# Expert loop written out, with eight gathered tiles and six sets of weights

## The chip, the cores and the metric

The kernel runs on one core of a Trainium2 chip. Its time is the device time of one execution in microseconds; the time before is the median of three runs. The profile is that of one further execution.

## The reference

Four layers follow one another, each added to a residual stream of 2 x 1024 tokens of 512 floats: attention with 16 heads, a feed-forward layer with FP4 weights, a linear recurrence, and a mixture of experts. The change touches the last alone:

```python
E, CAP, TOP_K, H, F = 64, 128, 6, 512, 352
scores = softmax(x @ gate_w.T)                    # in float32
topk_w, topk_idx = top_k(scores, TOP_K)
# the first CAP tokens that chose expert e stand in buf[e]; further ones are dropped
g = silu(einsum('ech,ehf->ecf', buf, w_gate))
u = einsum('ech,ehf->ecf', buf, w_up)
d = einsum('ecf,efh->ech', g * u, w_down)
y = sum over a token's six experts of topk_w * d  # zero where it was dropped
y = y + (silu(x @ sh_gate.T) * (x @ sh_up.T)) @ sh_down.T
```

Everything is float32.

## The kernel before

Six phases run one after the other, with a barrier of all engines between them: qkv, attention, FP4 feed-forward, recurrence, router with the shared expert, and the experts. The first five end near 1330 us of the profiled execution, and the change doesn't touch them. The router phase leaves the normalised token rows with their 64 scores behind them in DRAM (tensor xs, in the trace expert_rows: rows of XS = 576 floats), the result so far in DRAM (out, in the trace out_x), and in slot_rows, for each expert, the 128 rows of its slots. It also loads the weights of experts 0 and 1 (PREFETCHED = 2).

experts_phase (L1765) works on one expert after the other, in a step on each engine. The steps run at different times on different engines; semaphores tie them. With e the expert:

- POOL gathers the 128 rows of expert e into xg with an indirect DMA (L1842; row numbers from row_in), AHEAD = 4 experts ahead. When y of expert e is ready and the addition of expert e-1 has landed, it issues the scatter that adds y to out in DRAM, an indirect DMA with compute_op add (L1850; row numbers from row_out), and only then gathers for e+4 into the xg from which y(e) took its scores. The scatter's instruction on POOL raises add_begun; its landing raises added.
- SP loads the weights of expert e (2.16 MB in four DMAs: w_gate and w_up at L1399, w_down at L1404 and L1405) into one of R = 4 sets. It waits until the up product, the split of w_down and the beginning of the addition of expert e-4 are past (three waits, and then all four DMAs). The first loads also wait for three gathers.
- PE, in step e: four transposes of xg(e+1) into a bank (L1866, turn_x); gate, then up of expert e, four float32 products each, which the trace shows as eight matmul records each (L1886); the down product of expert e-1, three float32r products for each of three slices of F (L222 to L224, helper product3); three transposes of hidden(e) (L1895).
- ACT: silu of the gate bank (L1914); the high part of w_down (L1918); weigh(e-1), which writes y, in the trace e_y, from the down bank times the token's score (L1908); the high part of the turned hidden (L1924).
- DVE: copies the turned x out of its bank (L1943), copies a column of slot_rows to row_in for e+4 and to row_out for e (L1934, L1938), multiplies silu and up (L1954), and takes the low parts of w_down and the turned hidden (L1958, L1963).

There are two buffers each of xt, silu, hidden, the split parts and y. Function over_experts writes the first four and the last four steps out, and runs the 56 between in a hardware loop (Fori) of 14 rounds of four steps; in the loop waits against register values go through wait_apart (L411). Steps are numbered by the expert of their gate product, 0 to 63.

Of the kernel before, what the change touches and what calls it, by code (L numbers as in the profile page):

```python
# [13 lines left out]
P = 128  # L14
# [393 lines left out]


def wait_apart(engine, semaphore, value, passed):  # L410


    if not isinstance(value, int):
        value = engine.to_reg(value)  # L414
    engine.wait_ge(passed, 1)
    need(engine, semaphore, value)
# [978 lines left out]
def load_gate_up(sp, a, weights, e, loaded):  # L1395

    for w, name in zip(weights, ("w_gate", "w_up")):
        src = a[name][bass.ds(e, 1)].rearrange("o (p k) n -> p (o k) n", p=P)
        sp.dma_start(w[:, :, :], src).then_inc(loaded, 16)  # L1399


def load_down(sp, a, weights, e, loaded):
    w, src = weights[2], a["w_down"][bass.ds(e, 1)]
    sp.dma_start(w[:, 0:DOWN_FULL, :], src[:, 0:DOWN_FULL * P, :].rearrange("o (k p) n -> p (o k) n", p=P)).then_inc(loaded, 16)  # L1404
    sp.dma_start(w[0:F - DOWN_FULL * P, DOWN_FULL, :], src[:, DOWN_FULL * P:, :].rearrange("o p n -> p (o n)")).then_inc(loaded, 16)  # L1405
# [358 lines left out]
def experts_phase(nc, m, a):  # L1764
# [26 lines left out]
    y = [arena.put(f"e_y{i}", [P, D], F32) for i in range(2)]  # L1791
# [6 lines left out]
    gathered = [s(f"gathered{i}") for i in range(R)]  # L1798
# [6 lines left out]
    def exists(e):  # L1805
        return not isinstance(e, int) or 0 <= e < E

    def over_experts(engine, step):

        for e in range(R):  # L1810
            step(e, e, 0)
        with engine.Fori(1, GROUPS - 1) as g:
            for u in range(R):
                step(g * R + u, u, g)
        for e in range(E - R, E):
            step(e, e % R, GROUPS - 1)

    with nc.Block() as block:

        @block.sync  # L1820
        def _(sp):
            def step(e, u, g):
                if isinstance(e, int) and e < PREFETCHED:
                    return
                if isinstance(e, int) and e == PREFETCHED:
                    for i in range(R - 1):
                        sp.wait_ge(gathered[i], 16)

                need(sp, up_done, e - R + 1)
                need(sp, down_ready, e - R + 1)  # L1830
                need(sp, add_begun, e - R + 1)
                load_gate_up(sp, a, weights[u], e, gu_loaded[u])
                load_down(sp, a, weights[u], e, down_loaded[u])
            over_experts(sp, step)

        @block.gpsimd
        def _(pool):
            def gather(e, u):

                need(pool, y_ready, e - R + 1)  # L1840
                wait_apart(pool, row_in_ready, e + 1, row_in_ready)
# [3 lines left out]
            def step(e, u, g):  # L1845
# [15 lines left out]
        def _(pe):  # L1861
            def turn_x(e, u, g):
                pe.wait_ge(gathered[u], 16 * (g + 1))
# [5 lines left out]
            def down(e, u, g):  # L1869
# [3 lines left out]
                b = u % 2  # L1873
# [4 lines left out]
            def step(e, u, g):  # L1878
                if exists(e + 1):
                    turn_x(e + 1, (u + 1) % R, g if u < R - 1 else g + 1)  # L1880
                pe.wait_ge(xt_ready, e + 1)
                need(pe, gu_loaded[u], 32 * (g if u < PREFETCHED else g + 1))
                need(pe, hidden_ready, e - 1)
                for w, bank, done in ((w_gate, GATEB, gate_done), (w_up, UPB, up_done)):
                    for k in range(KT):
                        last = pe.matmul(m.bank[bank[u % 2]][:, 0:F], xt[u % 2][:, k, :], w[u][:, k, :],  # L1886
                                         start=(k == 0), stop=(k == KT - 1))
                    last.then_inc(done, 1)
                if exists(e - 1):
                    down(e - 1, (u - 1) % R, g if u else g - 1)  # L1890
                pe.wait_ge(hidden_ready, e + 1)
                need(pe, ht_ready, e)
                for k in range(GF):
                    r = rows[k]
                    last = pe.transpose(m.bank[HB][0:r, k * P:(k + 1) * P], hidden[u % 2][:, k * P:k * P + r], m.ident[:, :])  # L1895
                last.then_inc(h_turned, 1)

            turn_x(0, 0, 0)
            over_experts(pe, step)
            down(E - 1, R - 1, GROUPS - 1)  # L1900

        @block.scalar
        def _(act):
            def weigh(e, u):

                act.wait_ge(down_done, e + 1)
                need(act, added, 16 * (e - 1))
                act.activation(y[u % 2][:, :], m.bank[YB[u % 2]][:, :], ACT.Copy,  # L1908
                               scale=xg[u][:, bass.ds(D + e, 1)]).then_inc(y_ready, 1)

            def step(e, u, g):
                act.wait_ge(gate_done, e + 1)
                need(act, hidden_ready, e - 1)
                act.activation(silu[u % 2][:, :], m.bank[GATEB[u % 2]][:, 0:F], ACT.Silu).then_inc(silu_ready, 1)  # L1914
                need(act, down_loaded[u], 32 * (g if u < PREFETCHED else g + 1))
# [130 lines left out]
```

## Time and profile before

| | us |
|---|---|
| median of three runs | 2006.24 |
| lowest and highest | 2005.0, 2006.75 |
| profiled execution, its own time | 2010.12 |
| its span, first to last instruction | 2008.4 |

Busy time and share of the span, from the page:

```profile
PE 1742.8 (87%) x7201; PEld 1211.6 (60%) x7201; DVE 1101.6 (55%) x2379; ACT 693.6 (35%) x1316; POOL 575.7 (29%) x862
```

PE is the matrix engine, PEld its weight load, DVE the vector, ACT the scalar and POOL the GpSimd engine; SP only issues transfers. The page also cuts the span into 40 slices of 50 us: the tenths of each in which PE was busy, TensorE's granted clock in tenths of full speed, and the mean busy share of the 16 DMA engines. The expert loop fills the last 13 or so.

```profile
PE   6997999999888998988599999968888878888786
...
PEclk9996999999999988989799999989889899989888
DMA  6235456655215000000201100158878788787874
```

A share of busy time says little of what sets the pace. That is read from the chain of work that ended last, from the waits of each engine, and from the timeline; a DMA's time is given from its issue to its landing.

### The profile page before, as it was taken

To read this page: it belongs to the slowest core of one execution; us is meant where nothing else is said; L and a number is where in the kernel's file an instruction comes from. 1 tells how busy PE (TensorE), PEld (TensorE's weight loads), DVE (VectorE), ACT (ScalarE), POOL (GpSimd) and SP (SyncE) were. 2 spreads that over 40 slices of the span, in tenths; PEclk is the share of its full clock that TensorE was granted. 3 is DMA by queue.
4 is the path that set the end of the run, shared out by engine and by line. 5 is a ranking of instruction groups with operands and counts; after the bars stand their busy time and mean duration, and the time that the engine had idled before them with its cause. 6 is when DMAs were issued, how large, how long until landed. Compare 5 with 4: busy or idle time off the path is not lost. (4 is left out here: it accounts for less than half of the span.)

```text
span 2008.4 us, 23935 instructions
## 1 busy us (share of the span) xinstructions
PE 1742.8 (87%) x7201; PEld 1211.6 (60%) x7201; DVE 1101.6 (55%) x2379; ACT 693.6 (35%) x1316; POOL 575.7 (29%) x862
## 2 busy tenths in 40 slices
PE   6997999999888998988599999968888878888786
PEld 5884545554466666766477677745555555556564
DVE  5436667766357676765874787763333333333332
ACT  3120555555424534444324222213232223323232
POOL 2003233345503343333541311102222222222222
PEclk9996999999999988989799999989889899989888
DMA  6235456655215000000201100158878788787874
GB/s 246 95 145 154 135 147 169 173 149 150 68 44 195 1 1 1 1 0 21 82 1 62 44 19 35 57 201 268 259 242 284 248 272 269 258 268 242 275 256 130
DMA packets 120637, 284.50 MB, mean 142 GB/s; under 512 B 23456, under 2 KB 35232, under 8 KB 120288
## 3 DMA queue, kind: packets, MB, share of 16 engines
q1 hardware_dynamic: 106208, 247.71, 35.9%
q0 software_dynamic: 14336, 35.66, 8.7%
q8 instruction: 45, 0.74, 0.2%
q14 instruction: 48, 0.39, 0.1%
HBM read 224.03 MB, written 54.69 MB: 139 GB/s over the span
## 5 line engine op out<-in xcount | busy, mean ns | idle before, releaser
L1850 POOL DMA_INDIRECT out_x<-e_y,row_out x64 | 100.8, 1575 | 485.2 <-ACT e_y L1908 481.2
L839 ACT ACTIVATE probs<-bank 128x512 f32<-128x512 f32 (+3 forms) x384 | 167.6, 503 | 194.3 <-PE bank L787 192.8
L1886 PE MATMUL bank<-w_gate,xgt 128*128 128x352 f32 x512 | 208.0, 561 | 0.0
L1954 DVE TENSOR_TENSOR e_hidden<-e_silu,bank 128x352 f32<-128x352 f32 x64 | 33.4, 521 | 269.6 <-issue 219.0
L1105 PE MATMUL bank<-ln_xt_hi,gu_codes 128*128 128x512 f32 x352 | 149.7, 425 | 36.2 <-ACT gate_sum L1120 15.8
L762 PE MATMUL bank<-k_stack,q_stack 96*128 96x512 f32 (+3 forms) x384 | 147.3, 404 | 28.9 <-DMA k_stack<-qk_parts 15.7
L1886 PE MATMUL bank<-w_up,xgt 128*128 128x352 f32 x512 | 163.9, 463 | 0.0
L1866 PE MATMUL bank<-ident,xg 128*128 128x128 f32 x256 | 50.0, 324 | 116.7 <-DMA xg<-expert_rows,row_in 115.9
L1886 PEld LDWEIGHTS bank<-w_gate,xgt 128*128 128x128 f32 x512 | 115.0, 236 | 58.9 <-issue 31.8
L882 DVE CUSTOM_DVE_ANT_0 masked_scores<-bank,wide_mask 128x128 bf16<-128x128 f32 (+3 forms) x256 | 116.2, 483 | 58.1 <-PE bank L762 57.1
L787 PE MATMUL bank<-q_stack,k_stack 98*128 98x512 f32 (+3 forms) x384 | 141.6, 384 | 2.2 <-ACT probs L839 1.8
L801 PE MATMUL bank<-probs,v_ones 128*64 128x512 f32 (+3 forms) x768 | 142.5, 508 | 0.0
L1106 PE MATMUL bank<-ln_xt_lo,gu_codes 128*128 128x512 f32 x352 | 142.0, 403 | 0.0
L1914 ACT ACTIVATE e_silu<-bank 128x352 f32<-128x352 f32 x64 | 29.6, 463 | 324.4 <-PE bank L1886 324.4
L711 POOL TENSOR_SCALAR_AFFINE_SELECT probs<-probs 128x128 f32<-128x128 f32 x256 | 78.3, 322 | 205.7 <-ACT probs L839 201.6
L1886 PEld LDWEIGHTS bank<-w_up,xgt 128*128 128x128 f32 x512 | 101.0, 197 | 58.9 <-issue 8.3
L762 PEld LDWEIGHTS bank<-k_stack,q_stack 96*128 96x128 f32 x384 | 76.8, 202 | 66.5 <-DVE max_parts L882 19.6
L1105 PEld LDWEIGHTS bank<-ln_xt_hi,gu_codes 128*128 128x128 f32 x352 | 67.6, 192 | 81.3 <-ACT gate_sum L1120 21.9
L1958 DVE TENSOR_TENSOR e_down_lo<-w_down,e_down_hi 128x1024 fp32r<-128x1024 f32 (+1 forms) x128 | 116.2, 950 | 0.0
L1866 PEld LDWEIGHTS bank<-ident,xg 128*128 128x128 f32 x256 | 38.0, 210 | 125.1 <-issue 108.1
L1167 DVE SCALAR_TENSOR_TENSOR hidden<-bank,gu_scale,hidden 128x512 f32<-128x512 f32 x132 | 99.0, 750 | 15.5 <-ACT hidden L1120 3.9
L886 DVE TENSOR_REDUCE max_parts<-bank 128x1 f32<-128x512 f32 x128 | 82.5, 683 | 41.8 <-PE bank L762 41.8
(242 smaller groups left out, 3899.1 us busy)
## 6 DMA issues: line engine op xcount, KB each, us to landing
w_gate<-in_w_gate SPq DMA_DIRECT2D x64, 704.0 KB, 5.6
w_up<-in_w_up SPq DMA_DIRECT2D x64, 704.0 KB, 7.6
w_down<-in_w_down SPq DMA_DIRECT2D x64, 512.0 KB, 8.0
q_stack<-qk_parts SPq DMA_DIRECT2D x96, 128.0 KB, 3.9
k_stack<-qk_parts SPq DMA_DIRECT2D x96, 128.0 KB, 4.0
w_down<-in_w_down SPq DMA_DIRECT2D x64, 192.0 KB, 8.5
qk_parts<-qk_stage_hi SPq DMA_DIRECT2D x32, 256.0 KB, 2.0
qk_parts<-qk_stage_lo SPq DMA_DIRECT2D x32, 256.0 KB, 2.3
```

Source lines behind the costliest of these rows:

```text
L762: pe.matmul(m.bank[MAXB[at % 3]][:, 0:cols], qs[slot][j][0:ROWS, q * P:(q + 1) * P], ks[slot][j][0:ROWS, half * CH:half * CH + cols], star ...
L787: pe.matmul(bank[:, 0:cols], ks[slot][j][0:ROWS + 2, k * P:(k + 1) * P], qs[slot][j][0:ROWS + 2, q0:q0 + cols], start=True, stop=True).the ...
L801: pe.matmul(m.bank[OUTB[c]][j * 2 * HD:(j + 1) * 2 * HD, q0 - c * CH:q0 - c * CH + cols], vs[p % 2][j][:, k, :], probs[u % PROBS][:, 0:col ...
L839: act.activation(probs[u % PROBS][:, 0:cols], m.bank[EXPB[u % 3]][:, 0:cols], ACT.Exp, scale=scale).then_inc(exp_ready, 1)
L882: dve.tensor_tensor_reduce(out=masked[at % 4][:, 0:cols], in0=bank[:, 0:cols], in1=wide_mask[:, CH - cols:], scale=1.0, scalar=-3e38, op0= ...
L1105: pe.matmul(bank[:, :], gu[:, k, w], hi[:, k, :], start=True, stop=False)
L1106: pe.matmul(bank[:, :], gu[:, k, w], lo[:, k, :], start=False, stop=True).then_inc(product_done, 1)
L1167: dve.scalar_tensor_tensor(out=total[:, :], in0=m.bank[RING[at % 4]][:, :], scalar=gu_scale[:, half * G0 + g, k:k + 1], in1=total[:, :], o ...
L1850: pool.indirect_dma_start(out=a["out"][:, :], out_offset=bass.IndirectOffsetOnAxis(ap=row_out[u][:, :], axis=0), in_=y[u % 2][:, :], in_of ...
L1866: last = pe.transpose(m.bank[XB][:, k * P:(k + 1) * P], xg[u][:, k:D:KT], m.ident[:, :])
L1886: last = pe.matmul(m.bank[bank[u % 2]][:, 0:F], xt[u % 2][:, k, :], w[u][:, k, :], start=(k == 0), stop=(k == KT - 1))
L1958: last = dve.tensor_tensor(down_lo[u % 2][p, k, :], w_down[u][p, k, :], down_hi[u % 2][p, k, :].bitcast(F32), ALU.subtract)
```

## The change

The hardware loop is gone: each engine's 64 steps are written out, with constants for register values, and wait_apart is no longer needed. Gathers run eight experts ahead (AHEAD = 8, eight xg and row_in); a gather still comes behind the scatter of the expert whose xg it fills. There are six sets of weights (R = 6), and a load waits for up, down split and begun addition of expert e-6; SP asks for the addition first, and for down_ready only between the gate/up and the down loads. There are four y and four row_out (YS = 4), so weigh and the copy to row_out wait for the landed addition of expert e-4. The work of a step and its order on PE, ACT and DVE are as before. Its core:

```diff
+    R, AHEAD, YS = 6, 8, 4
...
-    R = 4
-    GROUPS = E // R
...
-    row_in = [arena.put(f"row_in{i}", [P, 1], U32) for i in range(R)]
-    row_out = [arena.put(f"row_out{i}", [P, 1], U32) for i in range(R)]
-    AHEAD = R
-    xg = [arena.put(f"xg{i}", [P, XS], F32) for i in range(R)]
+    row_in = [arena.put(f"row_in{i}", [P, 1], U32) for i in range(AHEAD)]
+    row_out = [arena.put(f"row_out{i}", [P, 1], U32) for i in range(YS)]
+    xg = [arena.put(f"xg{i}", [P, XS], F32) for i in range(AHEAD)]
...
-    y = [arena.put(f"e_y{i}", [P, D], F32) for i in range(2)]
+    y = [arena.put(f"e_y{i}", [P, D], F32) for i in range(YS)]
+    assert arena.at <= SBUF_END
...
-    def over_experts(engine, step):
-
-        for e in range(R):
-            step(e, e, 0)
-        with engine.Fori(1, GROUPS - 1) as g:
-            for u in range(R):
-                step(g * R + u, u, g)
-        for e in range(E - R, E):
-            step(e, e % R, GROUPS - 1)
+    def loads_of(e):
+
+        return e // R if e % R < PREFETCHED else e // R + 1
 
...
+            for i in range(3):
+                sp.wait_ge(gathered[i], 16)
+            for e in range(PREFETCHED, E):
+                u = e % R
+                need(sp, add_begun, e - R + 1)
                 need(sp, up_done, e - R + 1)
+                load_gate_up(sp, a, weights[u], e, gu_loaded[u])
                 need(sp, down_ready, e - R + 1)
-                need(sp, add_begun, e - R + 1)
-                load_gate_up(sp, a, weights[u], e, gu_loaded[u])
                 load_down(sp, a, weights[u], e, down_loaded[u])
-            over_experts(sp, step)
...
+            def gather(e):
+                u = e % AHEAD
+                need(pool, y_ready, e - AHEAD + 1)
+                pool.wait_ge(row_in_ready, e + 1)
...
-            def step(e, u, g):
-
+            for e in range(AHEAD):
+                gather(e)
+            for e in range(E):
                 pool.wait_ge(row_out_ready, e + 1)
                 pool.wait_ge(y_ready, e + 1)
-                wait_apart(pool, added, 16 * e, row_out_ready)
-                pool.indirect_dma_start(out=a["out"][:, :], out_offset=bass.IndirectOffsetOnAxis(ap=row_out[u][:, :], axis=0),
-                                        in_=y[u % 2][:, :], in_offset=None, compute_op=ALU.add,
+                need(pool, added, 16 * e)
+                pool.indirect_dma_start(out=a["out"][:, :], out_offset=bass.IndirectOffsetOnAxis(ap=row_out[e % YS][:, :], axis=0),
+                                        in_=y[e % YS][:, :], in_offset=None, compute_op=ALU.add,
                                         engine_sem=add_begun).then_inc(added, 16)
-                if exists(e + AHEAD):
-                    gather(e + AHEAD, (u + AHEAD) % R)
-            for e in range(AHEAD):
-                gather(e, e)
-            over_experts(pool, step)
+                if e + AHEAD < E:
+                    gather(e + AHEAD)
             pool.wait_ge(added, 16 * E)
...
-                need(act, added, 16 * (e - 1))
...
+                need(act, added, 16 * (e - YS + 1))
...
-                if not isinstance(e, int) or e >= R:
-                    wait_apart(dve, gathered[u], 16 * g, row_in_ready)
...
-                wait_apart(dve, added, 16 * (e - R + 1), row_in_ready)
...
+                need(dve, gathered[u], 16 * (e // AHEAD))
...
+                need(dve, added, 16 * (e - YS + 1))
```

## Rows read from the trace of the kernel before

**Rows 1.** Table of stretches: length; busy us per engine; clock, DMA share, GB/s.

```profile
1600.00:1700.00 100.00, 82.34 (x311) 57.63 (x310) 36.45 (x80) 28.55 (x58) 25.63 (x20) 0.91 0.81 260
```

**Rows 2.** Chain of work that ended last: start us, us, what ran or landed.

```profile
1582.52 0.70 ACT e_y L1908
...
1586.03 7.17 DMA xg<-expert_rows,row_in
...
1594.07 6.43 PE bank L1886 x16
1602.81 0.70 ACT e_y L1908
```

**Rows 3.** Waits of PE, 1339 to 1985: us in total, times, longest.

```profile
PE bank L1866 <- DMA xg<-expert_rows,row_in: 107.3, 30, 5.4
```

**Rows 4.** Timeline of PE, at steps 1 and 2, within the loop, step 63.

```profile
1346.75 2.53 PE L1886 MATMUL bank<-w_gate,xgt 128*128 128x352 f32 x8
...
1354.39 1.05 PE L1886 MATMUL bank<-w_gate,xgt 128*128 128x352 f32 x3
...
1603.24 2.53 PE L1886 MATMUL bank<-w_gate,xgt 128*128 128x352 f32 x8
...
1613.57 0.75 PE L1866 MATMUL bank<-ident,xg 128*128 128x128 f32 x4 [3.04 <-DMA xg<-expert_rows,row_in]
1614.16 4.22 PE L1886 MATMUL bank<-w_gate,xgt 128*128 128x352 f32 x8
...
1985.23 1.05 PE L1886 MATMUL bank<-w_gate,xgt 128*128 128x352 f32 x3
```

**Rows 5.** Table of stretches, 2 us each, between two bursts and within one.

```profile
1604.00:1606.00 2.00, 2.00 (x8) 1.26 (x8) 1.29 (x5) 0.19 (x1) 1.55 (x1) 1.00 0.00 0
1606.00:1608.00 2.00, 2.00 (x9) 1.26 (x8) 0.00 (x0) 1.73 (x3) 1.01 (x2) 1.00 0.77 86
...
1616.00:1618.00 2.00, 2.00 (x5) 1.21 (x4) 0.00 (x0) 0.00 (x0) 0.00 (x0) 0.50 1.05 387
```

**Rows 6.** Landings: gathers 1400 to 1980; all scatters; those of 1362.89 and 1966.25.

```profile
DMA to landing us min/median/max: 7.1/7.6/9.5
...
DMA to landing us min/median/max: 4.6/5.0/8.7
...
DMA to landing us min/median/max: 6.9/6.9/6.9
...
DMA to landing us min/median/max: 7.6/7.6/7.6
```

**Rows 7.** Weight loads: page's issues; q1 of 1339 to 1987; SP's first issue.

```profile
w_gate<-in_w_gate SPq DMA_DIRECT2D x64, 704.0 KB, 5.6
...
w_down<-in_w_down SPq DMA_DIRECT2D x64, 192.0 KB, 8.5
...
q1 hardware_dynamic: 41664, 134.10, 54.3%
...
q14 instruction: 3, 0.02, 0.0%
...
1339.05 0.34 SPq L1399 DMA_DIRECT2D w_gate<-in_w_gate  x1
```

**Rows 8.** DMA view of 1608 to 1622.6, in a burst: 40 slices, total.

```profile
GB/s 231 328 412 417 417 417 432 412 425 398 421 414 385 379 421 393 404 236 146 129 157 226 286 369 417 386 447 448 359 411 457 436 439 363 375 411 387 415 275 90
DMA packets 1693, 5.25 MB, mean 359 GB/s; under 512 B 188, under 2 KB 188, under 8 KB 1693
```

**Rows 9.** DMA view of 1994 to 2000, a scatter alone; chain's end.

```profile
q0 software_dynamic: 144, 0.26, 34.8%
...
1993.69 4.82 DMA out_x<-e_y,row_out
1998.57 0.71 issue
```

**Rows 10.** DMA view of 1339 to 1987: instruction queue, packets and MB.

```profile
q8 instruction: 3, 0.05, 0.0%
```

More of the change, by code:

```diff
@@ L1867, in turn_x, with down @@
                 last.then_inc(x_turned, 1)
-            def down(e, u, g):
+            def down(e):
                 pe.wait_ge(ht_ready, e + 1)
@@ L1876, in down @@
                           for k, r in enumerate(rows)]).then_inc(down_done, 1)
-            def step(e, u, g):
-                if exists(e + 1):
-                    turn_x(e + 1, (u + 1) % R, g if u < R - 1 else g + 1)
+            turn_x(0)
+            for e in range(E):
+                if e + 1 < E:
+                    turn_x(e + 1)
                 pe.wait_ge(xt_ready, e + 1)
-                need(pe, gu_loaded[u], 32 * (g if u < PREFETCHED else g + 1))
+                need(pe, gu_loaded[e % R], 32 * loads_of(e))
                 need(pe, hidden_ready, e - 1)
@@ L1894, in step, with weigh @@
                     r = rows[k]
-                    last = pe.transpose(m.bank[HB][0:r, k * P:(k + 1) * P], hidden[u % 2][:, k * P:k * P + r], m.ident[:, :])
+                    last = pe.transpose(m.bank[HB][0:r, k * P:(k + 1) * P], hidden[e % 2][:, k * P:k * P + r], m.ident[:, :])
                 last.then_inc(h_turned, 1)
-            turn_x(0, 0, 0)
-            over_experts(pe, step)
-            down(E - 1, R - 1, GROUPS - 1)
+            down(E - 1)
         @block.scalar
         def _(act):
-            def weigh(e, u):
+            def weigh(e):
@@ L1912, in step @@
+            for e in range(E):
                 act.wait_ge(gate_done, e + 1)
                 need(act, hidden_ready, e - 1)
-                act.activation(silu[u % 2][:, :], m.bank[GATEB[u % 2]][:, 0:F], ACT.Silu).then_inc(silu_ready, 1)
-                need(act, down_loaded[u], 32 * (g if u < PREFETCHED else g + 1))
+                act.activation(silu[e % 2][:, :], m.bank[GATEB[e % 2]][:, 0:F], ACT.Silu).then_inc(silu_ready, 1)
+                need(act, down_loaded[e % R], 32 * loads_of(e))
@@ L1916, in step @@
                 need(act, down_done, e - 1)
                 for p, k in TILES:
-                    last = act.activation(down_hi[u % 2][p, k, :], w_down[u][p, k, :], ACT.Copy)
+                    last = act.activation(down_hi[e % 2][p, k, :], w_down[e % R][p, k, :], ACT.Copy)
                 last.then_inc(down_hi_ready, 1)
-                if exists(e - 1):
-                    weigh(e - 1, (u - 1) % R)
+                if e >= 1:
+                    weigh(e - 1)
                 act.wait_ge(h_turned, e + 1)
@@ L1923, in step @@
                 for p, k in TILES:
[L1924 removed]
+                    last = act.activation(ht_hi[e % 2][p, k, :], turned_hidden[p, k, :], ACT.Copy)
                 last.then_inc(ht_hi_ready, 1)
[L1926 to L1927 removed]
+            weigh(E - 1)
         @block.vector
         def _(dve):
[L1931 to L1934 removed]
@@ L1951, in step @@
+            for e in range(AHEAD):
+                copy_row_in(e)
+            copy_x(0)
+            for e in range(E):
+                if e + 1 < E:
+                    copy_x(e + 1)
+                if e + AHEAD < E:
+                    copy_row_in(e + AHEAD)
+                copy_row_out(e)
                 dve.wait_ge(silu_ready, e + 1)
@@ L1962, in step @@
                 for p, k in TILES:
-                    last = dve.tensor_tensor(ht_lo[u % 2][p, k, :], turned_hidden[p, k, :],
-                                             ht_hi[u % 2][p, k, :].bitcast(F32), ALU.subtract)
+                    last = dve.tensor_tensor(ht_lo[e % 2][p, k, :], turned_hidden[p, k, :],
+                                             ht_hi[e % 2][p, k, :].bitcast(F32), ALU.subtract)
                 last.then_inc(ht_ready, 1)
-            for e in range(AHEAD):
-                copy_row_in(e, e, 0)
-            copy_x(0, 0)
-            over_experts(dve, step)
 PHASES = [qkv_phase, attention_phase, ffn_phase, recurrence_phase, router_phase, experts_phase]
```

68 lines of the change are left out of this document (22 added, 46 removed).

## The prediction

> **What bounds the kernel now.** I read the stretch table first: in the expert loop PE is busy 82 us in 100, and the DMA share is 0.81 [rows 1]. Neither is full, so a wait sets the pace. The chain that ended last shows it: the activation that writes e_y, 0.70 us, issue time on POOL and the scatter's own instruction, a gather xg that takes 7.17 us, four transposes, sixteen gate/up matmuls (and, not listed, the down product), and the next e_y [rows 2]. The next e_y comes 20.3 us later, but is that of the second expert after: gather(e+4) is issued behind scatter(e), turn_x(e+4) is step e+3's first work, and down(e+2), also in step e+3, makes y(e+2). One turn of the chain is two experts. The list of PE's waits agrees: 30 waits for xg, 107.3 us, and no other that reaches 1 us in the whole loop [rows 3].
>
> The timeline prices both kinds of step. Without a wait, gate starts 1346.75 and again 1354.39: 7.64 us, with PE always busy [rows 4]. With one, PE stands for 3.04 us in this instance, and the eight gate matmuls after it take 4.22 us in place of 2.53; the granted clock there is 0.50, the lower level, 1.2 GHz [rows 4, 5]. A pair is 2 x 7.64 + 3.04 + 1.69 = 20.0 us, against 20.3 on the chain. From step 1 (1346.75) to step 63 (1985.23) 62 steps take 638.5 us, **10.30 us each** [rows 4].
>
> **The change, part by part.**
>
> Gathers eight ahead, eight xg. Gather(e+8) still follows scatter(e), but has over seven steps until its transposes, some 55 us, against a landing of 9.5 us at the longest [rows 6]. The wait leaves the path for good, with the half-clock gate work after it: up to (10.30 - 7.64) x 62 = **165 us**. That would be all if nothing else came late.
>
> Four more gathers at the start. They are moved ahead of everything POOL does for step 0, some 1.25 us each (0.95 and 0.30 of issue). POOL's first scatter is due at 1355, the four would end at about 1343, and SP's first loads wait for gathers 0 to 2 only, which stay first. Cost on the path: 0. The same bytes, only earlier.
>
> Six sets of weights. Load(e) waits for the addition of expert e-6, which begins near the end of step e-5, so it has four steps, over 30 us, until step e; its parts land 5.6 to 8.5 us after their issue and SP takes about 2 us to issue it [rows 7]. The wait itself costs nothing. What takes its place is the transfers' throughput. SP can now keep up to four sets queued, so the engines should never run dry as they do today.
>
> That capacity is the term that decides. Today bursts of two experts' traffic stand between holes: share 0.00 at 1604 to 1606, 0.77 in the next stretch, and full until the slices fall off near 1622.4 [rows 5, 8]. From about 1606.4 that is 16.1 us for two experts, 8.05 each. The second way: mean share 0.81 x 10.30 = 8.3, a little high, as overlapping packets take some stretches above 1. The third is by parts: one set is 2.16 MB, 134.1 MB for 62 [rows 7]; at the 395 GB/s that loads reach amid a burst (slices of 390 to 430, [rows 8]) 5.5 us. A gather, 128 rows of 576 floats, is 0.295 MB: 0.75 us. A scatter with nothing beside it keeps the engines 34.8% of 6 us, 2.1 us, for 0.26 MB [rows 9]; amid loads it is the dip to some 150 GB/s near 1615 in [rows 8], which gives about 2 us too. Sum 8.3. I take **8.2 us an expert**, the middle of the three. That is above PE's 7.64, so I expect the transfers to bind, and PE to wait some 0.6 us a step for w_gate and w_up, each time far less than the 3.04 us that precede today's slow gate work.
>
> So step 63's weights arrive at 1339.4 (first load issued 1339.05, [rows 7]) + 62 x 8.2 - 1.8 (the last w_down, 0.72 MB, isn't needed for gate) = 1846.0, against 1985.2 today: **139 us** less. Bounds: 8.0 gives 152; 8.5 gives 121. Below 7.64 PE binds and it is 165.
>
> The loop written out. No loop branch and no register waits. A written-out step and a looped one take the same in this trace (head 7.64; looped: 1594.07 to 1603.24 is 9.17, less 1.69 of slow gate 7.5, [rows 2, 4]), so 0 gained. The code must be fetched now: queue q8 moved 3 packets of instructions, 0.05 MB, in the 648 us of the loop [rows 10]; 14 rounds written out may need 14 times as many, 42, and their 0.7 MB are nothing beside 2.7 MB an expert. A late one would stall its engine, and no row here shows a stage with written-out code and full queues. Upper bound: a third of the 42 are PE's and each holds it for the shortest landing of a load, 5.6 us [rows 7], 78 us, of which PE's spare 0.6 us a step (37 us) takes up half: 41 us. Lower bound 0, or a gain of the little that branches cost. I take 0: a fetch needn't wait for anything but its turn, and can be asked for long ahead.
>
> Four y, waits for additions three further back. The scatter itself still waits for the landing of the one before, so additions stay one after another. With idle transfer engines one takes 4.82 us to landing and 0.71 of issue [rows 9], 5.5 us. But the scatters of this loop come in two kinds [rows 6]. The first of a pair meets no loads and lands in 4.6 to 5.1 us. The second is issued into a full burst: asked one by one, the thirty from 1362.89 (6.9 us) to 1966.25 (7.6 us) average 6.84, at most 8.7. From now on all are of the second kind: 6.84 + 0.71 = 7.55 us an addition, below 8.2 but near it. It costs 0 so long as it stays below; four y and row_out let it swing by some steps. DVE's copy of row_out and the ACT activation wait for additions at least four back: 0. SP asks for add_begun before down_ready; when an addition has begun the other is long true, and nothing but loads is queued behind it: 0.
>
> The tail behind step 63's gate start, 23.2 us to the end of the span, stays. **Sum:** 2010.1 (profiled; span 2008.4 and 1.7 around it) - 139 = 1871. The median of the runs lies 3.9 us below the profiled one, so 2006.2 - 139 = **1867 us**.
>
> **The rivals.**
>
> *PE binds (0.13).* If a saturated pair of queues hides part of the scatter, an expert's traffic falls under 7.64 us. For it: 14.6 us of burst moved 5.25 MB at 359 GB/s [rows 8], and 2.72 MB at that rate is 7.6 us. Against: this stretch leaves out most of one scatter. Gain 165: 1841 us, and the clock then stays at 2.4 GHz throughout.
>
> *The chain of additions binds (0.25).* Today's second scatter has an idle stretch of the engines some microseconds on; with queues full all the time each may land like the longer ones. At 8.0 to landing, 8.7 a step, SP's add_begun holds the loads and ACT the y: gain 62 x 1.6 = 99, 1907 us; at the longest, 8.7 and 9.4 a step, gain 56, 1950. For it: the wide spread, 4.6 to 8.7 [rows 6]. Against: these scatters also had the gather of the pair's first expert just ahead, as they will have, and if additions lag, the loads thin out and the landing shortens. The Trainium skill has a rule that speaks for this rival: DMA: Bandwidth & Descriptors, section "Latency and other measured facts", gives the HBM access as 0.2 us on average and 2 us at high load. An add reads and writes HBM, so by it an addition may take up to 3.6 us more than the idle one, 5.5 + 3.6 = 9.1 us (an estimate from the page), and the time would be near 1930; the trace's 2 us between the two kinds of scatter lies within that.
>
> *Slower than before (0.02).* The same place with a higher price: a step costs more than today's 10.30 when a scatter lands in over 9.6 us. The loaded kind is 2 us above the idle one; if a queue of four sets in place of one or two added three times that again, to 12.8 and 13.5 a step, it would be + 62 x 3.2 = 198, 2204 us. None of the 64 scatters is near.
>
> *It doesn't do what it says (0.02).* If gathers still landed late (behind queued loads), PE's waits for xg stay: 2000. They would have to take 55 us.
>
> *Code (0.04).* Instruction fetches late behind full queues, at the upper bound: 1867 + 41 = 1908.
>
> **How the numbers follow.** The forecast, transfers bind at 8.0 to 8.5, has 0.54: 1854 to 1885. The range takes PE's bound (1841) at the low end, and at the high end the code case and most of the addition rival: 1838 to 1920, some 0.85. A difference of 0.2%, 4 us, is about what can be told from no change; every case but two is far beyond it: faster 0.96, same 0.02, slower 0.02.
>
> **What would show it.** Right: PE's wait for xg is gone but for the first; gate starts about 8.2 us apart after a lead of some steps at 7.64; DMA share 0.95 or more through the loop, over 320 GB/s, no holes; PE's remaining waits end on w_gate/w_up loads; granted clock near 1.0; scatters land in about 7 us. Wrong: gate starts 7.64 apart and DMA share below 1 (PE binds); scatter's waits for the landing before it, and SP waiting long for additions (the addition chain); PE idle for "issue" between groups of matmuls (code).

## The result, and the profile after

| | before | after |
|---|---|---|
| median, us | 2006.24 | 1883.96 |
| lowest and highest, three runs | 2005.0, 2006.75 | 1878.89, 1884.23 |
| profiled execution, its span | 2010.12, 2008.4 | 1878.89, 1877.0 |

The changed kernel takes 0.9384 of the time before (95% interval 0.9359 to 0.9409), 122 us less. The forecast was 1867 with a range of 1838 to 1920: the time lies in it, 17 us over the forecast. Started again in a later sitting, the same kernel had a median of 1879.0, so two sittings can differ by 5 us.

First the page: busy time, then three of the lines with 40 slices of 47 us.

```profile
PE 1693.2 (90%) x7201; PEld 1184.8 (63%) x7201; DVE 1097.0 (58%) x2379; ACT 697.1 (37%) x1316; POOL 623.2 (33%) x862
...
PE   6997999999997998898958999999799999999995
...
PEclk9997899999998999998978999999899999999998
DMA  7236356665423200000030021112699999999994
```

In the ten slices before the last, 1361 to 1830 us, TensorE's clock, PE's busy share and the DMA share are all at 9, that is 90% or more; before, the clock fell to 8 in some slices and the DMA share stood at 7 or 8. The table of stretches (columns as in [rows 1]) and the waits (us in total, times, longest) of 1345 to 1830 say what has taken the gather's place:

```profile
1500.00:1600.00 100.00, 93.42 (x388) 65.79 (x386) 43.17 (x96) 37.18 (x72) 40.96 (x24) 1.00 1.00 330
```

```profile
DVE row_out L1908 <- DMA out_x<-e_y,row_out: 220.0, 53, 6.5
POOL out_x L1826 <- DVE row_out L1908: 163.3, 39, 7.0
...
PE bank L1870 <- DVE e_hidden L1927: 21.5, 22, 2.0
```

PE's wait for xg [rows 3] is gone, and the slow gate work behind it. But PE waits for no weights either. What it waits for is e_hidden from DVE, and DVE stands 220 us in front of its copy of row_out, until an addition has landed; SP's waits before it loads, 332.8 us in all, are put down to additions too. The chain that ended last is, from 1500 us on, almost nothing but additions (compare [rows 2]):

```profile
1584.14 0.54 issue
1584.89 5.82 DMA out_x<-e_y,row_out
1590.78 0.54 issue
1591.53 8.99 DMA out_x<-e_y,row_out
1600.58 0.54 issue
1601.33 5.91 DMA out_x<-e_y,row_out
```

One after the other: 0.54 us of issue, 5.8 us to landing, again 0.54, and 9.0. The view of all scatters (duration on POOL in ns min/median/max, start of the first and the last) gives the mean distance from one start to the next: (1867.0 - 1354.1) / 63 = **8.14 us an addition**. Their landings:

```profile
L1826 POOL DMA_INDIRECT out_x<-e_y,row_out x64: 1545/2421/2576, 1354.1 to 1867.0; - x64
...
DMA to landing us min/median/max: 4.7/7.2/9.9
```

In the kernel before a scatter took 1.58 us on POOL, at most 1.62; here the median is 2.42.

```profile
L1850 POOL DMA_INDIRECT out_x<-e_y,row_out x64: 1545/1575/1622, 1355.3 to 1999.3; - x64
```

The timeline around one of the long ones shows its company:

```profile
1584.10 0.15 DVE L1908 COPY row_out<-slot_rows 128x1 uint32<-128x1 uint32 x1 [4.76 <-DMA out_x<-e_y,row_out]
...
1584.21 0.52 DVE L1927 TENSOR_TENSOR e_hidden<-e_silu,bank 128x352 f32<-128x352 f32 x1
...
1584.65 1.82 DVE L1931 TENSOR_TENSOR e_down_lo<-w_down,e_down_hi 128x1024 fp32r<-128x1024 f32 x2
...
1584.89 2.42 POOL L1826 DMA_INDIRECT out_x<-e_y,row_out  x1 [5.29 <-DVE row_out L1908]
...
1587.62 0.99 POOL L1817 DMA_INDIRECT xg<-expert_rows,row_in  x1 [0.30 <-issue]
```

The landing at 1584.1 releases two engines at once. DVE copies row_out, and the hidden product and e_down_lo (1.82 us) come straight behind; POOL issues the next scatter 0.24 us after e_down_lo has begun. 51 of the 64 scatters took more than 1.7 us, and every one was issued while e_down_lo ran.

The 1.82 us of e_down_lo are two instructions, x2 in the row; the view of the tile gives them as 1.22 us (128x1024) and 0.68 us (96x512):

```profile
L1931 DVE TENSOR_TENSOR e_down_lo<-w_down,e_down_hi x128: 678/950/1222, 1344.5 to 1852.1; 128x1024 fp32r<-128x1024 f32 x64, 96x512 fp32r<-96x512 f32 x64
```

The scatter above was issued 0.24 us into the first of the two and ended 1.45 us after that instruction's end.

### The profile page after: what moved, and what is told of

Same layout as the page of the kernel before. It is cut to its first block and busy times, and to the rows that moved or that the text cites. A ratio compares the mean times of both kernels' runs of the same rounds, so it can differ in the third digit from the quotient of the medians.

```text
span 1877.0 us, 22599 instructions
## 1 busy us (share of the span) xinstructions
PE 1693.2 (90%) x7201; PEld 1184.8 (63%) x7201; DVE 1097.0 (58%) x2379; ACT 697.1 (37%) x1316; POOL 623.2 (33%) x862
## 5 line engine op out<-in xcount | busy, mean ns | idle before, releaser
L1826 POOL DMA_INDIRECT out_x<-e_y,row_out x64 | 144.1, 2252 | 310.8 <-DVE row_out L1908 176.2
L1861 PE MATMUL bank<-w_gate,xgt 128*128 128x352 f32 x512 | 163.6, 463 | 0.0
L1908 DVE COPY row_out<-slot_rows 128x1 uint32<-128x1 uint32 x64 | 9.8, 152 | 228.5 <-DMA out_x<-e_y,row_out 228.5
L1861 PEld LDWEIGHTS bank<-w_gate,xgt 128*128 128x128 f32 x512 | 93.8, 193 | 41.4 <-issue 1.3
L778 PEld LDWEIGHTS bank<-q_stack,k_stack 98*128 98x128 f32 x384 | 73.6, 193 | 52.2 <-ACT probs L830 24.9
L1879 ACT ACTIVATE e_y<-bank,xg 128x512 f32<-128x512 f32 x64 | 44.0, 688 | 162.6 <-PE bank L224 162.6
L1889 ACT ACTIVATE e_down_hi<-w_down 128x1024 fp32r<-128x1024 f32 (+1 forms) x128 | 100.0, 832 | 0.0
```

The costliest lines, as they stand in the source:

```text
L778: pe.matmul(bank[:, 0:cols], ks[slot][j][0:ROWS + 2, k * P:(k + 1) * P], qs[slot][j][0:ROWS + 2, q0:q0 + cols], start=True, stop=True).the ...
L1861: last = pe.matmul(m.bank[bank[e % 2]][:, 0:F], xt[e % 2][:, k, :], w[e % R][:, k, :], start=(k == 0), stop=(k == KT - 1))
L1889: last = act.activation(down_hi[e % 2][p, k, :], w_down[e % R][p, k, :], ACT.Copy)
```

## The experiments

Ratios are to the kernel before, on the same chip in the same sitting; "an addition" is the mean distance of the scatters' starts.

| | ratio (95%) | us | an addition |
|---|---|---|---|
| changed kernel, again | 0.9363 (0.9299 to 0.9427) | 1879.0 | 8.10 |
| two_chains | 0.9333 (0.9309 to 0.9357) | 1869.9 | 7.89 |
| loads_free | 0.9624 (0.9587 to 0.9661) | 1930.9 | 8.91 |
| row_out8 | 0.9272 (0.9250 to 0.9294) | 1859.6 | 7.82 |
| written_out | 0.9849 (0.9827 to 0.9871) | 1973.9 | |
| lo_first | 0.9263 (0.9222 to 0.9303) | 1861.9 | 7.81 |
| no_gather | 0.9191 (0.9149 to 0.9233) | 1847.1 | 7.59 |
| ahead8_only | 0.9250 (0.9214 to 0.9287) | 1857.6 | 7.75 |
| sets6_only | 0.9856 (0.9815 to 0.9896) | 1975.9 | |
| ahead8_y4 | 0.9223 (0.9168 to 0.9278) | 1854.6 | 7.80 |
| pace_pe | 0.9592 (0.9526 to 0.9657) | 1921.1 | 8.60 |
| pace_pe_y8 | 0.9480 (0.9415 to 0.9544) | 1904.3 | 8.53 |

The theories: A, the serial additions are the bound; B, the transfer engines' capacity is (the forecast's view); C, it is the place of the wait on DVE, ahead of the hidden product, which holds PE; D, formed from the first results, the wait on DVE makes the additions longer, because it lines e_down_lo up with the next scatter; E, the gather in POOL's queue is what makes every second landing long.

### two_chains: two additions in flight

```diff
-                need(pool, added, 16 * e)
-                pool.indirect_dma_start(out=a["out"][:, :], out_offset=bass.IndirectOffsetOnAxis(ap=row_out[e % YS][:, :], axis=0),
+                need(pool, added[e % 2], 16 * (e // 2))
+                pool.indirect_dma_start(out=a["out" if e % 2 == 0 else "out2"][:, :], out_offset=bass.IndirectOffsetOnAxis(ap=row_out[e % YS][:, :], axis=0),
```

> The changed kernel, but the additions of odd experts go to a second DRAM tensor, which is never merged (that part of the result is left out); so each addition waits only for the landing of the one two experts back, and two are in flight. Same bytes, same loads, same gathers. Theory A (the chain of additions, each waiting for the landing before it, is the bound): gate starts 7.64 us apart almost throughout, DVE's waits on row_out gone, time 1845 to 1855. Theory B (the 16 engines' capacity for this mix of traffic is the bound, and the chain of additions only fills with what they can't do faster): steps stay at 8.1 to 8.2, DMA share 1.0 at some 335 GB/s, time 1870 to 1885.

The odd experts' part of the result is left out here. The time lies between the two forecasts: 9 to 14 us less than the changed kernel. DVE's wait is gone, as A says, but the steps fall only to some 8.0 us. Now ACT does wait for weights, and PE's weight load stands before the gate products, for something that the view can't name ("issue"):

```profile
ACT e_down_hi L1890 <- DMA w_down<-in_w_down: 27.4, 45, 1.2
PEld bank L1862 <- issue: 16.8, 41, 1.4
```

```profile
1600.00:1700.00 100.00, 96.95 (x398) 68.80 (x397) 44.84 (x102) 38.99 (x75) 32.05 (x25) 1.00 1.05 340
```

```profile
DMA to landing us min/median/max: 4.5/9.1/10.9
```

With two additions in flight each lands in 9.1 us, and 340 GB/s is all that passes, though the queue of loads never runs low: from issue to landing a load of w_gate takes

```profile
DMA to landing us min/median/max: 3.9/18.1/21.7
```

against 6.7 us in the changed kernel. So there is a capacity limit close by, at about 8.0 us a step for this order of the traffic. It isn't the changed kernel's: from 1400 us on the engines moved 330 to 334 GB/s there, and the next experiment passed 347 of the same traffic.

### row_out8: DVE's copy waits for an addition eight back

```diff
-    R, AHEAD, YS = 6, 8, 4
+    R, AHEAD, YS, RO = 6, 8, 4, 8
...
-    row_out = [arena.put(f"row_out{i}", [P, 1], U32) for i in range(YS)]
+    row_out = [arena.put(f"row_out{i}", [P, 1], U32) for i in range(RO)]
...
-                need(dve, added, 16 * (e - YS + 1))
-                dve.tensor_copy(row_out[e % YS][:, :], m.slot_rows[:, e:e + 1]).then_inc(row_out_ready, 1)
+                need(dve, added, 16 * (e - RO + 1))
+                dve.tensor_copy(row_out[e % RO][:, :], m.slot_rows[:, e:e + 1]).then_inc(row_out_ready, 1)
```

> The changed kernel with eight row_out in place of four, so that DVE's copy waits for an addition eight back. In the changed kernel DVE stood 228.5 us before this copy, with the hidden product queued behind it. Theories A and B: the wait moves to the next one on the additions, ACT's write of y (four buffers), and the time stays, 1875 to 1885. Rival C (the place of the wait on DVE, ahead of the hidden product, is what slows PE): 1850.

A and B were wrong here: four more 512-byte tiles give some 20 us. PE runs at 7.63 us a step, fully busy, up to step 51 (1737 us), on the sets that lie ready:

```profile
1500.00:1600.00 100.00, 100.00 (x423) 72.14 (x423) 46.73 (x105) 40.31 (x81) 34.86 (x27) 1.00 1.04 348
```

```profile
L1826 POOL DMA_INDIRECT out_x<-e_y,row_out x64: 1544/1577/2592, 1356.4 to 1849.1; - x64
...
DMA to landing us min/median/max: 4.6/7.0/9.7
```

This ends B for the changed kernel. An expert's traffic is 2.72 MB (2.16 of loads, 0.295 of gather, 0.26 of scatter); at 348 GB/s that is 7.8 us, not 8.2. It isn't PE's 7.63 either: loads and gathers come behind the additions, and PE eats up the lead that six sets give it. The last scatter starts at 1849.1, with PE done by 1834.7; the end is still set by the additions, only each takes 7.82 us in place of 8.14. Whether 7.8 is the chain of additions by itself, or full engines that make each landing long, no run separates: two_chains, without the chain, came to 8.0.

C doesn't follow. From a landing to the next scatter's start it is 0.83 us in the mean in the changed kernel, here and in the next run (scatters 9 to 58), so no engine that the wait holds stands in the chain; what differs is the landing, 7.35 us against 6.97 here. Why did the landings get shorter? With DVE held no more, its e_down_lo and the scatters run at unrelated moments, and 16 scatters are long in place of 51.

### lo_first: the hidden product stays behind the wait, e_down_lo goes before it

```diff
+                dve.wait_ge(down_hi_ready, e + 1)
+                for p, k in TILES:
+                    last = dve.tensor_tensor(down_lo[e % 2][p, k, :], w_down[e % R][p, k, :],
+                                             down_hi[e % 2][p, k, :].bitcast(F32), ALU.subtract)
+                last.then_inc(down_ready, 1)
                 copy_row_out(e)
                 dve.wait_ge(silu_ready, e + 1)
...
-                dve.wait_ge(down_hi_ready, e + 1)
-                for p, k in TILES:
-                    last = dve.tensor_tensor(down_lo[e % 2][p, k, :], w_down[e % R][p, k, :],
-                                             down_hi[e % 2][p, k, :].bitcast(F32), ALU.subtract)
-                last.then_inc(down_ready, 1)
```

> The changed kernel with DVE's order changed: e_down_lo (1.82 us) before the copy of row_out, in place of behind the hidden product. The copy still waits for the addition four back and still has the hidden product queued behind it, so PE is held as before. In the changed kernel 50 of the 64 scatters took 2.42 us on POOL, all of them with e_down_lo beside them, and the ones without took 1.57. Theory D (the copy's wait starts e_down_lo and the scatter at the same moment; the scatter gets 0.85 us longer each time, and so the chain of additions): the scatters take 1.57 again, an addition goes from 8.1 to some 7.6 us, 1855 to 1868. Theory C (holding the hidden product is itself the loss): 1875 to 1885.

D's time, and D's row:

```profile
L1826 POOL DMA_INDIRECT out_x<-e_y,row_out x64: 1545/1577/2355, 1360.2 to 1852.0; - x64
...
DMA to landing us min/median/max: 4.7/6.9/9.8
```

The additions take 7.81 us, a landing 7.00 in the mean, 16 scatters are long, and the median is 1.58. PE's steps are 7.76 us for the other order. But the move did more than was meant. The copy comes later in DVE's step now, behind ACT's e_down_hi, and by then the addition four back has landed:

```profile
DVE row_out L1908 <- DMA out_x<-e_y,row_out: 0.5, 1, 0.5
```

So in both runs the wait on DVE went together with the long scatters, and neither run alone tells C from D; the 0.83 us of the last section speak against C.

That a scatter is long because of e_down_lo needs no such run: the traces of all kernels show it, instruction by instruction. In row_out8 the two meet at other offsets than in the changed kernel:

```profile
1475.33 1.81 DVE L1931 TENSOR_TENSOR e_down_lo<-w_down,e_down_hi 128x1024 fp32r<-128x1024 f32 x2
...
1475.88 2.12 POOL L1826 DMA_INDIRECT out_x<-e_y,row_out  x1 [5.51 <-DMA out_x<-e_y,row_out]
...
1805.27 1.81 DVE L1931 TENSOR_TENSOR e_down_lo<-w_down,e_down_hi 128x1024 fp32r<-128x1024 f32 x2
...
1806.03 1.91 POOL L1826 DMA_INDIRECT out_x<-e_y,row_out  x1 [6.39 <-DMA out_x<-e_y,row_out]
```

Issued 0.55 us into e_down_lo the scatter takes 2.12 us, issued 0.76 us into it 1.91; both end 2.67 us after e_down_lo began, 1.45 us after the end of its first instruction. It is so throughout: of 205 scatters in all runs that were issued more than 0.2 us before the end of such a subtraction, 203 end 1.42 to 1.46 us after it, whatever the offset. Of 97 gathers, 96 end 0.86 to 0.87 us after it. In the three others the subtraction had begun at most 0.04 us before, and it was the subtraction that took longer, 1.27 to 1.29 us in place of 1.22. Scatters that had begun before the subtraction kept their 1.58 us, and so did 18 issued beside the hidden product and 9 beside e_ht_lo, each of which has one input in a bank. No run took e_down_lo away.

How the longer instruction makes the chain slower is less plain. 35 fewer long scatters at 0.85 us are 30 us, and the chain became 20 us shorter. In row_out8 the long scatters landed no later than the short ones, 6.8 against 7.0 us in the mean. But the gather and the loads behind a scatter are issued only when its instruction ends, and the next scatter that lands late finds the gather with 3.2 us to go in the changed kernel and with 2.5 in row_out8. This would explain it; no run varies it alone.

The Trainium skill names a possible mechanism: by SBUF — State Buffer, section "Who interferes with whom", a VectorE instruction with two inputs in SBUF contends with a GpSimd instruction that reads SBUF, what they contend for is locked exclusively, and the order of issue decides which of the two is blocked. e_down_lo is such an instruction (w_down and e_down_hi), and it had begun first; the hidden product, one of whose inputs is a bank, is not. The direction agrees, and so does the size: POOL is held until the instruction's end, 0.98 us of 1.22 were left, and the scatter is 0.84 us longer. The same place infers that descriptors need GpSimd's write side, which such an instruction leaves free, and takes this for the reason why a tensor_tensor didn't stall DMA; here it does hold up the instruction that issues one. Which access is held no run here shows.

### no_gather: gathers for the first eight experts only

```diff
-                if e + AHEAD < E:
-                    gather(e + AHEAD)
...
-                pe.wait_ge(gathered[u], 16 * (e // AHEAD + 1))
+                pe.wait_ge(gathered[u], 16)
...
-                if e + AHEAD < E:
-                    copy_row_in(e + AHEAD)
```

> The changed kernel with gathers for experts 0 to 7 only; later experts reuse those eight tiles (their rows are left out). 56 gathers of 0.295 MB go. In the changed kernel landings of additions alternate, 5.9 and 9.0 us; each second scatter is issued with a gather still under way in the same queue. Theory E: without gathers all land in some 6 us, 6.7 with the issue, PE's 7.64 binds: 1842 to 1850. If the alternation comes from the loads, landings keep two kinds, and the time is 1855 or more.

The rows of the later experts are left out. As E says, the long landings go. From 1400 to 1800 they are

```profile
DMA to landing us min/median/max: 4.7/5.1/7.3
```

with loads beside them in every step: 5.1 us in the median, little more than the idle one's 4.82 [rows 9]. In the changed kernel the scatter issued right after a short landing finds the gather of the last step with 3.2 us still to go and lands in 8.8 us in the mean; the one after a long landing finds it with 0.8 us to go and lands in 5.9. So the two kinds go with the gather. Whether they come from its place in POOL's queue, as E has it, or from its 0.295 MB, which are gone too (320 GB/s here in place of 333), this run doesn't tell. [Rows 6] had two kinds as well, and the prediction put them down to the loads. PE binds here, 7.63 a step, the last scatter at 1835.9. One thing the gathers don't explain: the first scatters, 1357 to 1390, landed in

```profile
DMA to landing us min/median/max: 8.5/8.9/9.2
```

with the last gather landed by 1352, but with the first four sets of loads queued. Loads alone can cost an addition some 4 us, then, and one set issued right behind it next to nothing.

### loads_free: loads don't wait for additions

```diff
-                need(sp, add_begun, e - R + 1)
```

> The changed kernel without SP's wait for the begun addition: a load waits only for the up product and the split of w_down of the expert that used the set. Theory A: the queue of loads is as deep all along as it is at the start, where the first seven additions landed in 8.1 to 9.2 us against a median of 7.2; at 8.8 + 0.8 = 9.6 us an addition the time rises to 1950 to 1975. Theory B (capacity): the engines are full either way, the order of the traffic changes, its sum doesn't: 1875 to 1885. A third view, that the loads come late because of this wait: 1850.

A's direction, less than its size: 52 us slower than the changed kernel. Scatters land in 8.1 us in the median, at most 11.3, DVE waits 291.6 us. So the wait that the loads had isn't a brake. But the reason given for A, a queue that stays deep, is not what came: it is deeper only at the start. From 1500 to 1850 us w_gate lands in 5.4 us in the median, 6.0 in the changed kernel, and yet the scatters land in 8 us, and for most of them the last gather has landed before they are issued. What has changed is the moment: w_gate and w_up are issued some 3 us before a scatter, and no longer right behind one. The run isn't clean, as its DVE waits make 52 scatters long too.

Where four sets are pending SP's own issue instructions get long, 3.76 us for one at 1345.90 of the changed kernel, against mostly 0.3 to 0.9 later.

```profile
1338.91 1.00 SPq L1396 DMA_DIRECT2D w_down<-in_w_down  x1
...
1345.90 3.76 SPq L1396 DMA_DIRECT2D w_down<-in_w_down  x1
```

### pace_pe and pace_pe_y8: loads follow PE

```diff
-                need(sp, add_begun, e - R + 1)
-                need(sp, up_done, e - R + 1)
+                need(sp, up_done, e - 2)
```

with eight row_out; pace_pe_y8 has five sets, eight y as well.

> Eight row_out, and loads paced by PE: load e is issued when the up product of expert e-3 is done, whatever the additions do. At the start two or three sets are queued in place of four. With the load of one set at a time beside them the first additions should come 7.6 to 8 us apart in place of 9.5 to 10, which brings the whole chain of additions forward by 10 us: 1845 to 1852, against 1860 of the version with eight row_out alone. If an addition's time goes by the traffic of its step alone and not by what is queued: 1858 to 1862.

> The same pacing with five sets of weights, eight y and eight row_out: neither ACT nor DVE ever waits for an addition, so PE runs at 7.64 us to the end. If the chain of additions sets the end, the time is that of pace_pe, within 3 us, only the tail behind PE is longer. If PE's waits for additions cost anything by themselves, up to 8 us less.

Both missed by 50 us and more. At most three sets are queued, yet the first additions come 8.6 to 10.8 us apart, and some later ones, one after another, 10.0. In pace_pe it is now ACT that stands before its write of y:

```profile
ACT e_y L1878 <- DMA out_x<-e_y,row_out: 236.4, 42, 7.8
```

```profile
L1825 POOL DMA_INDIRECT out_x<-e_y,row_out x64: 1545/1577/2565, 1353.6 to 1895.5; - x64
...
DMA to landing us min/median/max: 4.6/8.1/10.0
```

8.1 us is the same median as with loads free, though only two scatters are long on POOL. So neither the depth nor e_down_lo is it: what both runs have lost is that a load is issued right behind an addition. The runs don't say what in the queues makes that moment good; that stays open. With eight y, ACT never waits for an addition and the time is some 17 us better, still bound by additions of 8.53; they lag so far that PE waits for xg again (26.0 us in 26 waits), as a gather comes behind the scatter eight back.

### The changed kernel again, beside the parts

> The changed kernel itself, unedited, as the measure for the three beside it: 1878 to 1886. Its additions come 8.1 us apart, 50 of 64 scatters take 2.4 us on POOL.

0.9363 with a mean addition of 8.10 us and 48 long scatters: the pattern of the first run, so it isn't a matter of one execution.

### The parts alone

written_out is R, AHEAD, YS = 4, 4, 2 with four row_out (and SP's new order of waits); sets6_only is 6, 4, 4; ahead8_only 4, 8, 2 with four row_out; ahead8_y4 is

```diff
-    R, AHEAD, YS = 6, 8, 4
+    R, AHEAD, YS = 4, 8, 4
```

> The loop written out alone: four gathers ahead, four sets of weights, two y, four row_out, as in the kernel before. The prediction put this at 0: 2004 to 2008. If branches or register waits cost anything, up to 20 us less; if code fetches stall, more.

> Written out with six sets of weights and four y and row_out, but gathers four ahead. The chain from y through scatter and gather to the transposes is untouched: by it 1970 to 1980, as written out alone. Where the six sets make the queue deeper, the gather lands later, and it may be slower, up to 2000.

> Written out with eight gathers ahead, but four sets of weights, two y and four row_out. Written out alone gave 1974. The gather is off the path. If the gather's wait was nearly all of the gain: 1875 to 1900. SP's wait for the addition four back now gives a load two steps, some 15 us, for a landing of 9.7 us, less what the additions lag; two y hold ACT as soon as an addition lags by one. If these bind, steps of 8.5 to 9 us and 1900 to 1930.

> Eight gathers ahead and four sets of weights, as the run that had two y and gave 1858, but with four y. Theory D: with two y, ACT's write of y waits for the additions before DVE's copy of row_out does, so the copy never starts a scatter together with e_down_lo; with four y the copy, which waits for the addition four back, is the first to wait again. Then the scatters of 2.4 us come back, additions go to some 8.1 us, 1872 to 1886. If it was six sets of weights that cost the changed kernel its 25 us: 1855 to 1862.

*Written out alone* gives 31 us, where 0 was forecast. The chain is that of before, with a shorter POOL part:

```profile
1585.23 0.70 ACT e_y L1879
1585.95 0.54 issue
1586.71 1.58 POOL out_x L1826
1588.59 7.51 DMA xg<-expert_rows,row_in
```

From the start of e_y to the gather's issue it is 3.36 us here and 3.51 in [rows 2] (1582.52 to 1586.03). The gathers on the chain landed in 7.50 us in the mean, 7.76 before, and 19 of 31 gate blocks on it ran slow, 25 of 28 before, worth another 0.5 us a pair. Together 0.9 of the 1.2 us a pair (20.6 before, 19.4 now). I put the first down to the register waits and the branch, which these steps no longer have; none of the three has an experiment of its own. Code fetches grew from 3 packets on q8 [rows 10] to 16, not 42, and no wait of an engine shows them.

*Six sets alone* add nothing to that: 0.9856 against 0.9849.

*Eight gathers ahead* give the rest, 116 us, and more than the whole change: 1857.6 with two y and 1854.6 with four, four sets each. No complete kernel here has a lower median than these two, but row_out8 and lo_first are so near that the intervals show no difference. The forecast's worry, that two steps are too short for a load, is visible but small:

```profile
PE bank L1861 <- issue: 8.2, 11, 1.3
...
ACT e_down_hi L1889 <- DMA w_down<-in_w_down: 1.3, 2, 1.0
```

```profile
L1826 POOL DMA_INDIRECT out_x<-e_y,row_out x64: 1545/1577/2615, 1351.8 to 1843.5; - x64
```

D's forecast for ahead8_y4 (long scatters back, 1872 and more) fell, and with it the reason given for ahead8_only: in neither run does ACT or DVE ever wait for an addition. With four sets PE is held now and then before its gate products instead, so the additions never lag by four, and only four scatters are long. It is the six sets that let PE run ahead to where the copy of row_out is the next to wait. So the 21 to 26 us between 1858 and the changed kernel's 1879 to 1884 come from the six sets together with four row_out, not from either alone: with eight row_out the six sets are harmless (1859.6).

## Why the prediction was right, and where not

*The number was right, the mechanism under it not.* The forecast, at 0.54, had the transfers bind; what binds are the additions, the rival at 0.25. Neither PE's bound nor code stalls nor late gathers show.

*Right.* The gather's wait and the half-clock gate work go (PE's one long wait for xg is the first, 8.5 us; granted clock 1.00 in the stretches); the addition of landings and issue was named as the near bound; one load set's latency never shows.

*The term that was mis-sized twice.* Step 63's gate was forecast for 1846.0 and began at 1845.5, but by two errors that cancel, which is luck. The transfers were put at 8.2 us an expert and passed in 7.8 (row_out8, 347 to 348 GB/s); with the queue always full, in two_chains, in 8.0. The forecast took the bursts of the kernel before, and a DMA share of 1, as full; these two runs stood at shares of 1.03 to 1.05 from 1500 us on. And the additions were put at 7.55 us and took 8.14. Without the alignment they take 7.8, so the landing of 6.84 (7.0 measured) and the issue of 0.71 (0.83) were good to 0.3 us together; the rest, 0.35 us an addition, comes and goes with the long scatters. The prediction had this chain, as the rival, at 8.7 us; it measures 8.14. The forecast should have seen that 7.55 is only 0.1 below PE's own step: two chains of nearly equal length, and the landings of one vary between 5.8 and 9.0 us.

*The wait that was costed at nothing.* "DVE's copy of row_out ... wait for additions at least four back: 0" failed. The first additions stood some 9 to 10 us apart against PE's 7.64, so the lag of four was reached at the copy for expert 8, at 1401.32; all 56 copies from there on waited, with the hidden product behind. By the 0.83 us the wait as such cost the chain nothing, and something must wait for the additions; what cost 20 us, as far as the runs show, is that it lines e_down_lo up with the next scatter.

*The tail.* Forecast unchanged, 23.2 us; it is 31.5 (1845.5 to 1877.0), as three additions are still to land when PE is done at 1856.7. They drain at 5.5 to 5.7 us each. These 8 us are half of the 17 that the median lay over the forecast; the other half is that the median was put 3.9 us below the profiled run and lay 5.1 above it.

*Four more gathers and six sets, costed at 0 at the start.* The first eight additions started 8.9 to 10.0 us apart. In ahead8_only, with the same gathers but two sets to load at the start in place of four, it was 6.3 to 9.0; over the first six that is 8 us less, though the first of them started 4 us later. So the queued sets are what costs there, and a chain that is behind from the start has no slack to get it back.

*The loop.* 0 was wrong for the kernel before, 31 us. In the changed kernel the path that it shortened is no longer the bound; a loop with eight gathers ahead wasn't tried, so its share in the 122 us is open.

*The cause of the long landings.* The prediction has the second scatter land late for the full burst that it is issued into; without gathers, in no_gather, nearly all land early beside the same loads. That loads can do it too, the first scatters and loads_free show. The rule it weighed from the Trainium skill's DMA: Bandwidth & Descriptors, section "Latency and other measured facts", up to 3.6 us more for an addition at high load, gave 9.1 us an addition and some 1930 us. The mean landing here is 7.35 us, 2.5 above the idle one, and with loads issued right behind each scatter and no gathers it is 5.1, only 0.3 above. The up to 3.6 us were nearly reached with loads free (8.1), and passed behind the first four queued sets (some 4 us more).

## What to carry to other kernels

When a buffer or a longer lead takes a wait away, work out what the serial chain that stays (here one read-modify-write DMA after another) costs an iteration, and compare it with the busy engine's own step; if they are within a few tenths, the cushions between them and where each one's wait stands in an engine's order decide. More buffers in one place only move the first wait: here six sets of weights moved it from PE to a DVE copy that then marched in step with POOL's scatters, and four sets were faster. When an instruction that issues a DMA takes longer than it did, look which instruction of another engine was running when it started. A wait that looks superfluous, like the load's for the addition, can be what keeps a shared queue in a good order; take it away in an experiment before counting it as slack.

## What the runs showed of the hardware

- A scatter's instruction on POOL took 1.58 us alone. Issued while a float32 subtraction of DVE with both inputs in SBUF ran, it ended 1.45 us after that subtraction, up to 2.6 us in all; a gather's took 0.99 us alone, and ended 0.86 us after it. The one that began first kept its time.
- A scatter with add of 0.26 MB landed in 4.8 us on idle engines, 5.1 with one set of loads issued right behind it, 8.1 with loads issued at other moments (loads_free, pace_pe), 8.5 to 9.2 with up to four sets of loads queued, and 8.8 with a gather ahead of it that had 3 us to go.
- A direct load's issue on SP took mostly 0.3 to 0.9 us, and up to 3.76 us with four sets pending (5.74 with loads free, at 1406.09).
- Loads, gathers and scatters together passed at 348 GB/s with one addition in flight, and at 340 with two and a queue of loads that took 18 us to land.
